# One more tile of each four slabs fetched by single rows in two passes, at tile 15 instead of 25, and its node numbers loaded earlier

## The reference, cut to what matters

```python
def _gine_conv(x, src, dst, e, W1, b1, W2, b2):
    msg = jax.nn.relu(x[src] + e)
    agg = jax.ops.segment_sum(msg, dst, num_segments=x.shape[0])
    h = x + agg
    h = jax.nn.relu(h @ W1 + b1)
    return jax.nn.relu(h @ W2 + b2)

e = jax.nn.relu(edge_attr @ W_l0 + b_l0) @ W_l1 + b_l1
h = relu(_gine_conv(x, src, dst, e, W00, b00, W01, b01))      # pass conv0
h = relu(_gine_conv(h, src, dst, e, W10, b10, W11, b11))      # pass conv1
x = _layernorm(x + h)
...
message = jnp.concatenate([x[row], x[col], edge_feat], axis=1)  # pass last
message = _mlp(message, W_msg, b_msg, g_msg, beta_msg)
agg = jax.ops.segment_sum(message, col, num_segments=node_feat.shape[0])
x = _layernorm(x + (agg + node_feat))
```

## Time and profile before

| | |
|---|---|
| median of 3 runs | 12169.41 us |
| the profiled execution's own time | 12147.42 us |
| its span in the profile | 12145.6 us |
| busy: PE, DVE, ACT, POOL | 9517.2, 7496.3, 4877.3, 9065.5 us |
| share of the span | 78%, 62%, 40%, 75% |
| granted TensorE clock, mean | 0.667 |
| POOL's first and last gather, `conv0` | 2.79 and 4023.11 us |
| `conv1` | 4044.82 and 8030.89 us |
| `last` | 8069.17 and 12075.32 us |

### The profile page before, as it was taken

One profiled execution on the slowest core, in us unless ns is written; L12 is line 12 of the kernel. 1 busy time (PEld: TensorE's weight loads), 2 busy tenths in 40 slices (PEclk: granted clock), 3 DMA queues, 4 the chain that ended last, 5 costly groups with the idle time before them and its releaser, 6 DMA issues. The chain is left out here.

```text
span 12145.6 us, 187868 instructions
## 1 busy us (share of the span) xinstructions
PE 9517.2 (78%) x34164; PEld 6796.1 (56%) x34164; DVE 7496.3 (62%) x15605; ACT 4877.3 (40%) x11020; POOL 9065.5 (75%) x9632
## 2 busy tenths in 40 slices
PE   5877777777777788899999999977777777777777
PEld 3655555555555555566666666655555555555555
DVE  5544444444444555566666666667777777777777
ACT  2333333333333344444444444444444444444444
POOL 6777777777777777777777777767777777777776
PEclk9999999999999655555555555555555555555555
DMA  3222222222222222222222222222222222222222
GB/s 93 48 48 47 48 50 48 48 50 48 49 49 48 67 51 52 52 56 57 56 57 56 57 56 57 55 52 53 52 54 53 53 53 53 54 53 53 54 52 56
DMA packets 606301, 651.29 MB, mean 54 GB/s; under 512 B 437595, under 2 KB 438200, under 8 KB 604745
## 3 DMA queue, kind: packets, MB, share of 16 engines
q0 software_dynamic: 306528, 471.44, 18.7%
q1 hardware_dynamic: 247141, 144.39, 5.0%
q10 hardware_dynamic: 51712, 27.54, 0.8%
HBM read 604.75 MB, written 39.45 MB: 53 GB/s over the span
## 5 line engine op out<-in xcount | busy, mean ns | idle before, releaser
L1382 PE MATMUL ps_pre<-w_e,conv_hid 97*128 97x96 f32 x12896 | 3270.7, 433 | 1171.9 <-DVE conv_part L667 1159.9
L1382 PEld LDWEIGHTS ps_pre<-w_e,conv_hid 97*128 97x128 f32 x12896 | 2877.0, 327 | 1917.6 <-issue 1301.0
L1382 PE MATMUL ps_pre<-last_w_q,last_hid 128*128 128x96 f32 x6448 | 1627.2, 432 | 1090.6 <-issue 513.5
L1382 PEld LDWEIGHTS ps_pre<-last_w_q,last_hid 128*128 128x128 f32 x6448 | 1440.3, 327 | 1478.8 <-issue 773.7
L649 ACT ACTIVATE conv_part<-ps_pre 128x384 bf16<-128x384 f32 x1736 | 815.8, 470 | 3541.2 <-DVE ps_pre L708 3530.3
L285 POOL DMA_INDIRECT early_got<-p_rows,early_idx x1612 | 1521.1, 944 | 533.9 <-issue 460.7
L285 POOL DMA_INDIRECT early_got<-in_x_rows,early_idx x1612 | 1524.4, 946 | 524.3 <-issue 440.6
L673 PE MATMUL ps_win<-conv_part,conv_hot 128*112 128x288 bf16 x6448 | 1906.1, 446 | 0.6 <-DVE conv_part L667 0.5
L285 POOL DMA_INDIRECT early_got<-h_rows,early_idx x1612 | 1521.5, 944 | 512.1 <-issue 450.8
L285 POOL DMA_INDIRECT last_got<-p_rows,early_idx x1581 | 1493.9, 945 | 482.0 <-issue 431.1
L285 POOL DMA_INDIRECT conv_got<-in_x_rows,early_idx x1581 | 1491.8, 944 | 483.1 <-issue 423.1
(11 more groups left out here) (256 smaller groups left out, 10741.8 us busy)
## 6 DMA issues: line engine op xcount, KB each, us to landing
conv_got<-in_x_rows SPq DMA_DIRECT2D x3968, 0.4 KB
conv_got<-h_rows SPq DMA_DIRECT2D x3968, 0.4 KB
last_got<-p_rows SPq DMA_DIRECT2D x3968, 0.4 KB
conv_row<-ea_parts SPq DMA_DIRECT2D x372, 84.5 KB
last_row<-ea_parts SPq DMA_DIRECT2D x372, 84.5 KB
early_got<-in_x_rows,early_idx POOLq DMA_INDIRECT x1612
early_got<-h_rows,early_idx POOLq DMA_INDIRECT x1612, 2.5
early_got<-p_rows,early_idx POOLq DMA_INDIRECT x1612
```

Source lines behind the costliest of these rows:

```text
L1382: mm = pe.matmul(ps["pre"][q % 2][:, t * C:(t + 1) * C], hid[q % 2][0:P if last else C1, t * P:(t + 1) * P], w_q[j % U][:, c * C:(c + 1) * ...
```

## The change

The one hand tile of each iteration (slab 3, tile 25) becomes slab 3, tile 15, in all three passes, with its rows in portions of 16, 64 and 48 instead of 48, 48 and 32. In `conv0` and `conv1` a second hand tile is added, slab 2, tile 15, whose rows are fetched at j = 0 (64) and j = 1 (64). POOL gathers 102 tiles of 104 there instead of 103. Since `HAND` has two entries, `load_hand_nodes` now loads two sets of node numbers, and it stands ahead of `store_near` and the constants instead of behind them.

```diff
-HAND = [(V - 1, T - 1, ((1, 0, 48), (2, 48, 96), (3, 96, P)))]
-HAND_OF = {"conv0": 1, "conv1": 1, "last": 1}
+HAND = [(V - 1, 15, ((1, 0, 16), (2, 16, 80), (3, 80, P))), (V - 2, 15, ((0, 0, 64), (1, 64, P)))]
+HAND_OF = {"conv0": 2, "conv1": 2, "last": 1}
...
                         for to, src in hid_loads:
                             sp.dma_start(to[:], src).then_inc(s["hf"], 16)
+                        prep.load_hand_nodes(sp)
                         prep.store_near(sp, s)
                         for to, src in consts:
                             sp.dma_start(to[:], src).then_inc(s["const"], 16)
-                        prep.load_hand_nodes(sp)
                         sp.wait_ge(s["nearout"], 16)
                         sp.wait_ge(s["set_fits"], 1)
```

## The result

The changed kernel takes 12186.22 us (median of 20 runs, 12177.89 to 12191.21), the kernel before 12166.83 beside it on the same chip (20 runs). The ratio is 1.0015, interval [1.0009, 1.0021]: 0.15% slower, inside the 0.2% that was called "same". The profiled execution of the kernel before, 12147.42 us, is not one of the 20 beside it, of which none took less than 12165.05.

The account below looks back on a forecast made before the run. POOL was taken to keep time, its gathers 1.248 us apart. The terms −76.1 + 58.9 + 29 + 11 − 20.5 = +2.3 on the profiled 12147.4, with the median 22 above, gave 12172 us; range 12130 to 12200.

Parts of the forecast that it names:

- A: Gathers saved on POOL in `conv0` and `conv1`: 61 at 1.248 us each, −76.1 us.
- Rival 5: PE or DVE takes POOL's place with its own waits, no gain in `conv1`: +38; chance 0.12 together with rival 3.
- B: Opening of `conv0`: two sets of numbers and 96 more rows delay slab 0's index list and POOL, +58.9 us.
- the alternative in the prediction: DMA engines alternate between queues packet by packet, so the numbers creep forward beside the load of `sums`.
- the case of 123: Opening of `conv0`: the numbers' loads progress undisturbed from 47.3, putting the last constant at 123 instead of 150 to 151.
- C: Catching up in `conv0`: POOL stalls 31 us at iteration 3 instead of 2.2, +29 us, unsure from 0 to +35.
- Rival 4: The catch-up stall in `conv0` costs nothing, as the compute reaches iteration 3 in time: 29 less, 12143; chance 0.07.
- D: Opening of `conv1`: more single rows delay the products POOL waits for, +11 us, bounds 0 and +16.
- E: Pass `last`: the moved tile removes POOL's wait once per iteration at chunk 2's third tile, −20.5 us.
- rival 2: `last` keeps its waits, chunk 6 simply ending one gather later: sum +23, 12193 us; chance 0.14.
- Rival 1: The numbers' loads in the opening of `conv0` are mostly hidden: 36 to 48 lower, 12124 to 12136; chance 0.17.
- Rival 3: SP bounds the conv passes, from 0.41 us per row: +260 at 0.43, some 12235 at 0.42; chance 0.12 with rival 5.

Follow-up runs that it names:

- Experiment 3: The changed kernel with the second hand tile in `conv1` alone, so one (tile 15) in `conv0`: 12125.47 us, ratio 0.9982 to the kernel before.
- experiment 9: The changed kernel with each set of node numbers loaded as two DMAs, 30 rows and 1 row: 12128.60 us, ratio 0.9980 to the kernel before.
- Experiment 11: The changed kernel with two index lists of `conv0`'s iteration 1 loaded ahead of single rows instead of behind: 12176.07 us, ratio 1.0019 to the kernel before.
- experiment 2: The kernel before with only the hand tile moved from 25 to 15 of slab 3: 12126.27 us, ratio 0.9982 to the kernel before.

## Why the prediction came out right

**A holds.** POOL stayed the metronome: 61 gathers, 76.1 us. Experiment 3 shows it in `conv1` alone (39 less 12 for the opening, 26 measured). Rival 5, PE or DVE taking over, did not come in.

**B holds, +61.8 for +58.9.** The last constant came at 152.28 (150 to 151 predicted), the first row at 163.65 (161.5), the list at 222.90 (219.8). Its reasoning, that the numbers all but stand still while `sums` is loaded, is borne out by the changed kernel's packets: five of 7936 start between 50 and 70 us (experiment 9). They do go in turn with the packets of `sums`, as the alternative in the prediction had it, but at one number for each 51,200 bytes, so the case of 123 did not come. The row's price was read a little low, 0.383 from runs of 48, where 64 and 80 in a run cost 0.39: 1.3 us of the 2.9. What was not seen is a second way: the compute begins behind the constants too, and with few rows ahead it is the compute that holds the list (experiment 3).

**C holds in size, +33.1 for +29, but not as a term of its own.** Experiment 11 took 31 us off the stall at the list and got them back as waits at later lists and at iteration 3. The chain of rows sets the sum B + C; every microsecond by which the first row comes earlier counts, and an earlier list with the same rows does not. Rival 4, no stall at iteration 3, is refuted by the 36.3 there.

**D +12.6 for +11, E −18.3 for −20.5.** D took POOL's second gather of iteration 1 behind 103 others, 4174.64; the one that waits is the first, behind 102, which in the trace of before would start at 4172.1. The release was put 1.3 late as well (140.8 us behind the pass's first gather, 139.5 measured), so the size came out near in part by luck. E is confirmed by itself in experiment 2, which also refutes rival 2.

**What the sum lacked.** By the traces it is +10.5 without the distance of gathers, and the 20 runs differ by 19.4. B, C, D and E were all put too low, by 2.9, 4.1, 1.6 and 2.2. Of the 9 that are left, 5.9 can be that the profiled execution was faster than the median of its runs. A part of that can be the first row: the five traces with the same preparation have it at 163.65, 166.76, 167.10, 168.89 and 171.95, so the profiled execution was an early one, and the changed kernel's runs spread over 13 us where those of before spread over 6. Whether the longer distance of gathers is in part of the 20 runs stays open. The forecast of 12172 was 14 below the 12186.2 measured. That "same" was right is owed to large terms that nearly cancel, with the sum right by 17 us; the signs and sizes of the terms are what the traces confirm.

**Rival 1 (loads hidden)** came near to being true only once they were spread and stood behind the constants (6.94 us). **Rival 3 (SP as the bound)** did not happen where the prediction was timed, with rows at 0.39, and did on another chip, with rows at 0.60 to 0.80, above the 0.41 to 0.42 from which the prediction had SP as the bound: 1.0998. On that chip the forecast would have been wrong, and nothing in the trace of before announced it.

## What to carry to other kernels

Where one engine keeps time, write the account by stalls of that engine and look for what fixes the end of the last of them: two stalls on one chain are one cost, and taking the first away alone gains nothing. Before moving a load into an apparent gap of an engine that issues, look at whether its queue is free and how many DMA engines the load's shape gives it; here two DMAs a set instead of one (30 rows and 1) brought the first row 34 us forward and turned 1.0015 into 0.9980. Price a change pass by pass: the same second tile saves 26 us in `conv1` and costs 38 in `conv0`, and the sum of the two hid it. And a move of work to a second issuing engine should be priced on more than one chip.

## What was not expected of the hardware

A single row issued by SP costs 0.39 us whether or not POOL gathers, in four of five sets of runs. On the chip of the fifth it cost 0.39 with POOL at rest in the opening and 0.60 to 0.80 beside gathers in the runs shown, and the kernel before, with one hand tile, took 14972 us there instead of 12148. The distance between gathers of the same program lay at 1.2480 and 1.2487 on two chips, and at 1.2507 for other programs beside the first.

Beside a load of 51,200-byte packets on ACT's queue, the 4-byte packets of SP's queue went at 1 (31 rows) or 15 and 1 (30 rows and 1) in about 4 us. Without it, 31 rows went at one packet every 6 ns.
